# One decoder layer on one core: the rotation folded into q, projections through one bank, a third feed-forward bank, two-byte turns and another order of the stages

## Chip, cores and metric

One core of one Trainium2 chip runs the kernel alone. The metric is the device time of one execution in microseconds (us), as the median of several runs; lower is better.

## What is computed

Input x has 16 tiles of 128 tokens with 256 channels, in f32; a second input `ctx` has the same shape. Each tile goes through three parts, each followed by a layer norm of (input + part). Cut to what matters:

```python
# 1. attention over heads: for every token, its 16 heads attend to each other
q, k, v = (x @ w.T).reshape(b, s, 16, 16)          # for wq, wk, wv
q, k = apply_rope(q, inv_freq), apply_rope(k, inv_freq)
scores  = einsum('bshd,bstd->bsht', q, k) / 4      # per token s: heads h by heads t
attn    = einsum('bsht,bstd->bshd', softmax(scores), v) @ wo.T
# 2. wkv: a recurrence over the 128 tokens of a tile, with k = the normed x, v = ctx
y_t = (e1 * aa + e2 * v_t) / (e1 * bb + e2)        # aa, bb decay by exp(-exp(time_decay))
# 3. feed-forward with quantised activations (127 steps) and ternary weights, 256 -> 704 -> 256
h   = silu(bitlinear(x, w1)) * bitlinear(x, w2);  out = bitlinear(h, w3)
```

`apply_rope` turns the pairs of channels of a token by angles that depend on the token's place alone. q and k of one score belong to the same token, so they are turned by the same angles.

## The kernel before, in words

The program is written engine by engine: one in-order instruction list each for TensorE (`block.tensor`), ScalarE (`block.scalar`), GpSimd (`block.gpsimd`), VectorE (`block.vector`) and the DMA queue of SyncE (`block.sync`), with semaphores between them. All lists run the same outer loop, `run_steps` (L75): `STEPS` = 16 tiles + `DEPTH` 5 = 21 steps. In step s a stage written `on(at(d), stage)` works on tile s - d. The order of the `on` lines in each engine's `step` function is the order of its instructions in a step, and nothing else sets it; `due` starts one-time work (the rounding of the feed-forward weights to ternary) at its place in the first steps.

A tile goes through these stages:

- Attention. `project_qk` (L387) makes q and k, 512 columns, in the bank `ps_qk`; `project_v` (L396) makes v in `ps_vt`. `rope` (L857, VectorE) multiplies q and k by the cosines and by the sines, `rotate` (L708, GpSimd) takes the difference and the sum of these products into `qk_rot`, and `to_dmajor` (L866, VectorE) transposes it in 32x32 blocks, twice 512 columns. `copy_v` (ScalarE), `v_to_dmajor` (VectorE), `block_v` (TensorE, four turns) and `copy_v_blocks` (ScalarE) lay v out for the last product. `score` (L409) makes the scores of all heads of four tokens at once, with a mask in spare rows. `max_quads` and three small instructions find each row's maximum, `shift` (L431) subtracts it by matmuls, `exp_scores`, `weigh_v` (twice 16 small matmuls), `heads_to_tokens`, `recip_sums`, `normalise`, `turn_attn`, `copy_attn` and `project_out` finish. `residual`, `moments`, `mean_var` (VectorE), `inv_std` (L761, GpSimd, three instructions) and `layernorm` (ScalarE) are used for all three norms.
- Wkv. `turn_k`, `exp_k` (four ACTIVATEs), `weigh_past` and `weigh_now` (GpSimd), `scan` (L945, VectorE), `add_now` (GpSimd). The division is done for two neighbouring tokens at once: `pair_dens` (L740) multiplies their denominators, `recip_den` (L951, VectorE) takes 128 reciprocals a partition, `cross_terms` (L746) and `divide` (L752) multiply. `turn_y` gives it back.
- Feed-forward. `amax_of_x`, `floor_x`, `recip_x` (VectorE) and `ffn_scales` (GpSimd) give the scales. `scale_x` (ScalarE) adds the constant MAGIC, which rounds to whole numbers; `turn_xq` (L488, two f32 turns) and `copy_xq`, which takes MAGIC off again, give bf16. `up` (L495) makes gate and up values in `ps_a` and `ps_b`, in two halves of 352 columns; `tanh_gate`, `copy_up` (ScalarE), `gate_up` (L974, VectorE) and `hidden` (L771, GpSimd) follow for each half. `amax_of_h`, `floor_h`, `recip_h`, `scale_of_h`, `scale_of_out` (VectorE), `scale_h` (ScalarE), `turn_hq` (L508, six f32 turns into `ps_a` and `ps_b`), `copy_hq` (two ACTIVATEs) and `down` (L515, into `ps_b`) end it. `up` of the next tile waits for `residual` 2 of this one, which reads `ps_b`.

On SyncE, a step issues, in this order, the load of xT (for this step's tile), of ctx (for three tiles back), of x (one back) and the store of the result (five back); each waits until its buffer is free. The weights come before the loop and in step 1.

## Time and profile before

| | |
|---|---|
| median of 3 runs | 296.25 us (295.87 to 297.29) |
| the profiled execution, its own time | 293.11 us |
| its span, first to last instruction | 291.1 us |
| mean granted TensorE clock | 0.86 |
| TensorE busy (matmuls) | 223.6 us, 77% |
| VectorE busy | 228.6 us, 79% |
| GpSimd busy | 184.7 us, 63% |
| ScalarE busy | 163.2 us, 56% |

How to read it: all engines work at the same time, so the shares don't add up to the span. Busy is the time between an instruction's start and its end in the record; neighbouring records of one engine can overlap, so the time from one start to the next is what an instruction costs in the queue. PE is TensorE, PEld its weight loads, DVE is VectorE, ACT is ScalarE, POOL is GpSimd, SP is SyncE. TensorE's granted clock is 1.0 at 2.4 GHz and 0.5 at 1.2 GHz.

### The profile page before, as it was taken

The numbers are of one execution on the slowest core, as the hardware profiler recorded it, in microseconds if no ns is written. First come the engines' busy times: TensorE is split into PE (matmuls) and PEld (weight loads), VectorE is DVE, ScalarE is ACT, GpSimd is POOL, SyncE is SP. The second block draws the span as 40 slices with busy tenths as digits, with TensorE's granted clock in tenths as the row PEclk, the third lists the DMA queues.
The fourth block names the chain that finished last, engine by engine and source line by source line (L and its number), as shares of the span: only waits on it lengthen the run. The fifth ranks groups of instructions, "written<-read, shape, count | busy, mean of one in ns | idle before, by whom it ended". The sixth has DMA issues, their size and how long they took to land.

```text
span 291.1 us, 9999 instructions
## 1 busy us (share of the span) xinstructions
PE 223.6 (77%) x3778; PEld 151.4 (52%) x3778; DVE 228.6 (79%) x557; ACT 163.2 (56%) x345; POOL 184.7 (63%) x384
## 2 busy tenths in 40 slices
PE   3462996979989898999888989898988785553622
PEld 1341765656655656667656666666665553321211
DVE  2686466688999999999999999999999977564221
ACT  2206232446767768485858585767576756544341
POOL 2203116577797979696779778697979777774311
PEclk9859586889999999797999999999999979755555
DMA  7900101010020202020202020202011000100000
GB/s 210 334 0 2 38 5 52 24 35 23 2 69 9 74 2 78 2 74 2 74 3 75 3 74 3 74 2 74 25 55 39 21 21 18 37 1 20 0 18 18
DMA packets 11968, 12.34 MB, mean 42 GB/s; under 512 B 1872, under 2 KB 11152, under 8 KB 11920
## 3 DMA queue, kind: packets, MB, share of 16 engines
q1 hardware_dynamic: 11200, 11.67, 12.7%
q8 instruction: 30, 0.49, 0.7%
q14 instruction: 18, 0.15, 0.2%
q10 hardware_dynamic: 720, 0.03, 0.2%
HBM read 9.60 MB, written 2.10 MB: 40 GB/s over the span
## 4 chain that ended last, share of the span: by engine, by line
DVE 25%; PE 24%; issue 20%; POOL 17%; ACT 7%; DMA 3%; SPq 1%; DVEq 0%; POOLq 0%; ACTq 0%
PE ps_s L425 6%; POOL hid L775 5%; PE ps_b L518 5%; DVE quad_max L884 4%; DMA w_raw<-w_in 3%; POOL qk_rot L712 3%; DVE qkD L871 3%; POOL qk_rot L711 3%; DVE gate L978 3%; POOL rstd L766 3%; PE ps_qk L393 3%; DVE qk_cos L862 2%; PE ps_a L505 2%; PE ps_b L505 2%; DVE qk_sin L862 2%
## 5 line engine op out<-in xcount | busy, mean ns | idle before, releaser
L393 PE MATMUL ps_qk<-wqkv,xT 128*128 128x512 f32 x64 | 35.6, 686 | 4.8 <-DMA wqkv<-wqkv_in 4.8
L622 ACT ACTIVATE th<-ps_a,half_gate 128x352 f32<-128x352 f32 x32 | 17.7, 553 | 35.1 <-PE ps_b L505 35.1
L734 POOL TENSOR_TENSOR frac<-state,now 128x512 f32<-128x512 f32 x16 | 20.3, 1268 | 24.2 <-DVE state L948 24.2
L425 PE MATMUL ps_s<-qkD 20*64 20x64 f32 x1024 | 25.2, 242 | 10.8 <-DVE qkD L871 7.5
L775 POOL TENSOR_TENSOR hid<-gate,up_s 128x352 f32<-128x352 f32 x32 | 29.7, 931 | 3.7 <-ACT up_s L627 1.6
L425 PEld LDWEIGHTS ps_s<-qkD 20*64 20x64 f32 x1024 | 20.9, 150 | 16.4 <-DVE qkD L871 7.2
L766 POOL TENSOR_TENSOR rstd<-var_eps,minus_half 128x1 f32<-128x1 f32 x48 | 26.3, 549 | 3.8
L586 ACT ACTIVATE probs<-ps_s 128x512 f32<-128x512 f32 x32 | 18.6, 591 | 16.0 <-PE ps_s L440 16.0
L871 DVE STREAM_TRANSPOSE qkD<-qk_rot 128x512 f32<-128x512 f32 x32 | 20.9, 691 | 6.5 <-POOL qk_rot L712 5.5
L643 ACT ACTIVATE x<-res,nmr,rstd 128x256 f32<-128x256 f32 x32 | 19.3, 603 | 10.5 <-POOL nmr L768 10.5
L978 DVE SCALAR_TENSOR_TENSOR gate<-th,ps_a 128x352 f32<-128x352 f32 x32 | 16.1, 502 | 11.4 <-ACT th L622 11.4
L399 PE MATMUL ps_vt<-wqkv,xT 128*128 128x256 f32 x64 | 19.0, 421 | 5.6 <-ACT v_blk L580 5.6
L458 PE MATMUL ps_o<-probs,v_blk 64*32 64x64 f32 x1024 | 22.2, 227 | 1.0 <-ACT probs L586 0.9
L505 PE MATMUL ps_a<-w,xqT 128*128 128x352 bf16 x64 | 16.7, 347 | 7.6 <-DVE gate L978 4.2
L393 PEld LDWEIGHTS ps_qk<-wqkv,xT 128*128 128x128 f32 x64 | 13.6, 228 | 15.6 <-issue 14.1
L763 POOL TENSOR_TENSOR var_eps<-mv,eps 128x1 f32<-128x1 f32 x48 | 9.2, 191 | 19.6 <-DVE mv L940 19.1
L711 POOL TENSOR_TENSOR qk_rot<-qk_cos,qk_sin 128x256 f32<-128x256 f32 x16 | 11.5, 718 | 15.1 <-DVE qk_sin L862 15.1
L458 PEld LDWEIGHTS ps_o<-probs,v_blk 64*32 64x32 f32 x1024 | 17.1, 112 | 7.3 <-issue 6.9
L935 DVE BATCH_NORM_STATS2 stats<-res 128x6 f32<-128x256 f32 x48 | 20.3, 424 | 0.7
L440 PEld LDWEIGHTS ps_s<-neg_eye,max_hi 128*64 128x64 bf16 x512 | 17.4, 114 | 6.4 <-issue 6.4
L948 DVE TENSOR_TENSOR_SCAN state<-w_tab,past 128x516 f32<-128x516 f32 x16 | 20.5, 1280 | 0.1
L884 DVE TRANSPOSE_TENSOR_REDUCE quad_max<-ps_s 128x32 f32<-128x1024 f32 x16 | 19.8, 1240 | 0.5 <-PE ps_s L425 0.5
(115 smaller groups left out, 629.7 us busy)
## 6 DMA issues: line engine op xcount, KB each, us to landing
xT<-xT_in SPq DMA_DIRECT2D x16, 128.0 KB, 2.4
x_res<-x_in SPq DMA_DIRECT2D x16, 128.0 KB, 2.3
ctxT<-ctxT_in SPq DMA_DIRECT2D x16, 128.0 KB, 2.2
out<-y_out SPq DMA_DIRECT2D x16, 128.0 KB, 1.7
w_raw<-w_in SPq DMA_DIRECT2D x2, 704.0 KB, 7.1
wqkv<-wqkv_in SPq DMA_DIRECT2D x2, 384.0 KB, 4.0
w_raw<-w_in SPq DMA_DIRECT2D x1, 640.0 KB, 8.8
wo<-wo_in SPq DMA_DIRECT2D x1, 256.0 KB, 5.1
```

What stands on the lines that cost most here:

```text
L393: last = mm(ps_qk[:], xT[k.slot][:, h, :], wqkv[:, h, 0:2 * C], start=h == 0, stop=h == 1)
L425: last = mm(ps_s[64 * half:64 * half + 64, g % 2, col:col + BLK], kk, q, start=(g < 2 and b < 2), stop=False, skip_group_check=True)
L458: last = mm(ps_o[PAD * g:PAD * g + PAD, dst:dst + BLK], v_blk[k.slot][rows, jj, g, :], probs[rows, g % 2, src:src + BLK], start=True, stop ...
L505: last = mm(bank[:, 0:FH], xqT[:, h, :], w12[:, h, i, cols], start=h == 0, stop=h == 1)
L734: g.tensor_tensor(frac[:].rearrange("p i h n -> p (i h) n"), state[:].rearrange("p i h n -> p (i h) n")[:, :, 0:P], now[:].rearrange("p i ...
L766: g.tensor_tensor(rstd[i][:], var_eps[i][:], minus_half[:], ALU.pow).then_inc(rstd_done[i], 1)
L775: g.tensor_tensor(hid[:, half * FH:(half + 1) * FH], gate[half][:], up_s[half][:], ALU.mult).then_inc(hid_done, 1)
L871: last = v.transpose(qkD[k.slot][:, i].rearrange("p (y h l) -> p h y l", h=HEADS, l=2), by_head[:, i])
L884: v.tensor_reduce(quad_max[:].rearrange("p s c -> p (s c)"), ps_s[:].rearrange("p b (c x) -> p (b c) x", x=PAD), AX.X, ALU.max, apply_tran ...
L935: v.bn_stats(stats[i][:], res[i][:]).then_inc(stats_done[i], 1)
L948: v.tensor_tensor_scan(flat(state), flat(w_tab), flat(past), 0.0, ALU.mult, ALU.add).then_inc(scanned, 1)
L978: v.scalar_tensor_tensor(gate[half][:], th[half][:], 1.0, ps_a[:, 0:FH], ALU.add, ALU.mult).then_inc(gate_done, 1)
```

## The change

What it does, by part:

- Rotation. Turning q and k by the same angles multiplies their product by cos^2 + sin^2 of each channel pair. `turn_gain` holds that factor per token and channel, `copy_q` (VectorE) multiplies q by it while copying it out of the bank, and k is only copied. `rope`, `rotate` and the tiles `qk_cos`, `qk_sin`, `qk_rot` go.
- One bank `ps_qkv` for q (256 columns), then k and v (512 columns), then the turned v blocks, in turn. ScalarE copies k and v together. All three are transposed on VectorE as before, now as three instructions in three places.
- Wkv: `pair_dens` and `cross_terms` go, `recip_den` takes 256 reciprocals a partition, and `divide` is one product.
- A third feed-forward bank `ps_c` holds the turned h and the result of `down`. `up` 0 waits for `copy_up` 1 and (through `turn_xq`) `gate_up` 1 of the tile before, and `turn_hq` for its `residual` 2.
- `whole_x` and `whole_h` (GpSimd) take MAGIC off into bf16, and the turns of xq and hq move bf16. `copy_xq` and `copy_hq` are plain copies, the second in one ACTIVATE.
- `DEPTH` 6: 22 steps. The stages stand in another order in all five lists, with other tile offsets.
- The DMA of the pads goes last on ScalarE's queue, and waits on constants moved from before the loops into the first tile of the stages that need them. Some counting semaphores are split in two.

The diff, cut:

```diff
-U_CUT = 50.0
+U_CUT = 60.0
-DEPTH = 5
+DEPTH = 6
...
-            def project_qk(k):
+            def project_q(k):
                 wait(pe, ld_xT[k.slot], 16 * (k.pair + 1))
-                wait(pe, rope_products, k.t)
+                wait(pe, v_blocks, k.t)
...
+                    last = mm(ps_q, xT[k.slot][:, h, :], wqkv[:, h, 0:C], start=h == 0, stop=h == 1)
+                last.then_inc(q_projected, 1)
+
+            def project_kv(k):
+                wait(pe, q_copied, k.t + 1)
                 for h in range(HALVES):
-                    last = mm(ps_v, xT[k.slot][:, h, :], wqkv[:, h, 2 * C:3 * C], start=h == 0, stop=h == 1)
-                last.then_inc(v_projected, 1)
+                    last = mm(ps_kv, xT[k.slot][:, h, :], wqkv[:, h, C:3 * C], start=h == 0, stop=h == 1)
+                last.then_inc(kv_projected, 1)
...
             def block_v(k):
-                wait(pe, v_dmajor, k.t + 1)
+                wait(pe, v_turned, k.t + 1)
+                wait(pe, kv_copied, k.t + 1)
...
             def turn_xq(k):
-                wait(pe, x_scaled, k.t + 1)
-                wait(pe, hqT_ready, k.t)
+                wait(pe, x_whole, k.t + 1)
+                wait(pe, gate_done[1], k.t)
                 for h in range(HALVES):
-                    last = turn(ps_a[:, h * P:(h + 1) * P], xq32[:, h * P:(h + 1) * P])
+                    last = mm(ps_xq[:, h * P:(h + 1) * P], xq16[:, h * P:(h + 1) * P], ident16[:],
+                              start=True, stop=True, is_transpose=True)
...
             def up(k, half):
                 if half == 0:
                     wait(pe, xqT_ready, k.t + 1)
-                    wait(pe, res_done[2], k.t)
+                    wait(pe, up_copied[1], k.t)
...
             def turn_hq(k):
-                wait(pe, h_scaled, k.t + 1)
+                wait(pe, h_whole, k.t + 1)
+                wait(pe, res_done[2], k.t)
...
             def down(k):
...
-                    last = mm(ps_b[:, 0:C], hqT[:, c, :], w3[:, c, :], start=c == 0, stop=c == FCH - 1)
+                    last = mm(ps_c[:, 0:C], hqT[:, c, :], w3[:, c, :], start=c == 0, stop=c == FCH - 1)
...
-            def rotate(k):
-                wait(pool, rope_products, k.t + 1)
-                wait(pool, qk_dmajor, k.t)
-                g.tensor_tensor(qk_rot[:, :, 0:HH], qk_cos[:, :, 0, :], qk_sin[:, :, 1, :], ALU.subtract)
-                g.tensor_tensor(qk_rot[:, :, HH:HD], qk_sin[:, :, 0, :], qk_cos[:, :, 1, :],
-                                ALU.add).then_inc(rotated, 1)
...
+                g.tensor_tensor(yT[:], frac[:, 1], den_rec[:], ALU.mult).then_inc(y_ready, 1)
...
+            def whole_h(k):
+                wait(pool, h_scaled, k.t + 1)
+                wait(pool, hq_turned, k.t)
+                g.tensor_scalar(hq16[:, 0:HIDDEN], hq32[:], -MAGIC, 1.0, ALU.add, ALU.mult).then_inc(h_whole, 1)
...
-            def rope(k):
-                wait(dve, qk_projected, k.t + 1)
-                wait(dve, rotated, k.t)
-                src = ps_qk[:].rearrange("p (g i) -> p g i", i=HH)
-                for dst, tab in ((qk_cos, cos_t), (qk_sin, sin_t)):
...
+            def copy_q(k):
...
+                wait(dve, q_projected, k.t + 1)
+                wait(dve, q_dmajor, k.t)
+                v.tensor_tensor(qkv_tok[:, 0, :, 0:HD].rearrange("p h (a i) -> p h a i", i=HH),
+                                ps_q.rearrange("p (h a i) -> p h a i", a=2, i=HH),
+                                turn_gain[:].unsqueeze(1).unsqueeze(1).broadcast_to([P, HEADS, 2, HH]),
+                                ALU.mult).then_inc(q_copied, 1)
...
             def recip_den(k):
-                wait(dve, pairs_done, k.t + 1)
+                wait(dve, frac_done, k.t + 1)
                 wait(dve, y_ready, k.t)
-                v.reciprocal(den_rec[:], den_pair[:]).then_inc(den_recips, 1)
+                v.reciprocal(den_rec[:], frac[:, 0]).then_inc(den_recips, 1)
```

The new order of a step, each list from first to last, with the tile offset in brackets (one-time work left out; its places: FFN weights' DMA in step 0; weight sums in VectorE's step 1 behind the transpose of k, TensorE's sum in step 2 ahead of the scores, the scales at the end of VectorE's step 1, rounding in ScalarE's step 1, cuts in VectorE's step 2, ternary weights in GpSimd's step 2):

- TensorE: project_kv (1), project_out (3), shift (2), block_v (1), turn_xq (5), weigh_v 0 (2), up 0 (5), weigh_v 1 (2), project_q (0), turn_hq (6), turn_y (4), up 1 (5), down (6), turn_k (3), score (1), turn_attn (2)
- VectorE: mean_var 1 (4), copy_q (0), gate_up 1 (5), q_to_dmajor (0), residual 2 (6), max_quads (1), amax_of_x (4), max_rows (1), floor_x (4), max_hi_part (1), recip_x (4), max_lo_part (1), scan (3), turn_v (0), amax_of_h (5), residual 0 (2), floor_h (5), recip_h (5), moments 0 (2), scale_of_h (5), mean_var 0 (2), recip_den (3), k_to_dmajor (0), gate_up 0 (4), moments 2 (6), heads_to_tokens (1), mean_var 2 (6), residual 1 (3), recip_sums (1), moments 1 (3), scale_of_out (5), normalise (1)
- ScalarE: copy_kv (0), scale_x (4), exp_scores 0 and 1 (1), copy_xq (4), copy_v_blocks (0), scale_h (5), tanh_gate 0 (4), copy_up 0 (4), copy_hq (5), layernorm 0 (2), tanh_gate 1 (4), copy_up 1 (4), layernorm 2 (6), exp_k (2), layernorm 1 (3), copy_attn (1)
- GpSimd: hidden 1 (5), weigh_past (3), weigh_now (3), whole_x (4), add_now (3), ffn_scales (4), inv_std 0 (2), whole_h (5), divide (3), hidden 0 (4), inv_std 2 (6), inv_std 1 (3)
- SyncE: xT (-1, the next tile's), store (6), x (0), ctx (1)

## Rows read from the trace of the kernel before

**Rows 1.** stretches: us, busy PE PEld DVE ACT POOL, PEclk, DMA share, GB/s.

```profile
176.03:189.72 13.69, 12.44 (x237) 8.45 (x236) 13.29 (x35) 9.70 (x22) 11.16 (x24) 1.00 0.13 41
259.00:273.00 14.00, 6.63 (x25) 3.37 (x24) 6.00 (x17) 5.88 (x11) 6.34 (x16) 0.50 0.03 11
```

**Rows 2.** timeline of VectorE, one middle step: start us, us, instruction.

```profile
177.33 0.42 DVE L935 BATCH_NORM_STATS2 stats<-res 128x6 f32<-128x256 f32 x1
177.66 0.48 DVE L896 CAST max_hi<-row_max 128x16 bf16<-128x16 f32 x1
...
178.55 0.94 DVE L954 RECIPROCAL den_rec<-den_pair 128x128 f32<-128x128 f32 x1
...
179.44 0.67 DVE L862 TENSOR_TENSOR qk_cos<-ps_qk,cos_t 128x512 f32<-128x512 f32 x1
...
180.64 0.50 DVE L978 SCALAR_TENSOR_TENSOR gate<-th,ps_a 128x352 f32<-128x352 f32 x1
181.06 0.41 DVE L923 TENSOR_TENSOR res<-ps_o,x_res 128x256 f32<-128x256 f32 x1
181.51 0.43 DVE L935 BATCH_NORM_STATS2 stats<-res 128x6 f32<-128x256 f32 x1
181.97 0.18 DVE L940 BATCH_NORM_AGGREGATE mv<-stats 128x2 f32<-128x6 f32 x1
182.23 0.89 DVE L984 TENSOR_REDUCE amax_h<-hid 128x1 f32<-128x704 f32 x1
183.16 0.21 DVE L991 TENSOR_SCALAR c_h<-amax_h,s_h 128x1 f32<-128x1 f32 x1
183.40 0.16 DVE L996 RECIPROCAL rec_h<-c_h 128x1 f32<-128x1 f32 x1
183.48 0.42 DVE L926 TENSOR_TENSOR res<-ps_w,x 128x256 f32<-128x256 f32 x1
183.82 0.20 DVE L1001 TENSOR_SCALAR s_h<-rec_h,s_h 128x1 f32<-128x1 f32 x1
```

**Rows 3.** VectorE's groups, whole run: busy us, mean ns of one | idle before.

```profile
L954 DVE RECIPROCAL den_rec<-den_pair 128x128 f32<-128x128 f32 x16 | 15.1, 941 | 0.0
...
L910 DVE RECIPROCAL o_rec<-o_tok 128x16 f32<-128x16 f32 x16 | 3.8, 236 | 0.0
```

**Rows 4.** timeline of TensorE, the middle step before that.

```profile
170.41 0.44 PE L385 MATMUL ps_w<-ident,x 128*128 128x128 f32 x2 [0.74 <-ACT x L643]
...
172.48 0.69 PE L425 MATMUL ps_s<-qkD 20*64 20x64 f32 x32 [0.20 <-DVE qkD L871]
...
174.00 0.83 PE L518 MATMUL ps_b<-w,hqT 128*128 128x256 bf16 x6
174.86 0.44 PE L385 MATMUL ps_a<-ident,xq 128*128 128x128 f32 x2
175.14 0.60 PE L385 MATMUL ps_vt<-ident,vD 128*128 128x128 f32 x4
```

**Rows 5.** GpSimd's groups, whole run.

```profile
L711 POOL TENSOR_TENSOR qk_rot<-qk_cos,qk_sin 128x256 f32<-128x256 f32 x16 | 11.5, 718 | 15.1 <-DVE qk_sin L862 15.1
...
L744 POOL TENSOR_TENSOR den_pair<-frac 128x128 f32<-128x128 f32 x16 | 6.4, 399 | 0.1
...
L794 POOL TENSOR_SCALAR w<-w_raw 128x1408 bf16<-128x1408 f32 x2 | 2.7, 1363 | 2.2 <-DVE w_raw L1026 2.2
```

**Rows 6.** VectorE's score maxima 1, 5, 16, residuals 2 of the last two tiles.

```profile
19.09 1.25 DVE L884 TRANSPOSE_TENSOR_REDUCE quad_max<-ps_s 128x32 f32<-128x1024 f32 x1
...
78.10 1.24 DVE L884 TRANSPOSE_TENSOR_REDUCE quad_max<-ps_s 128x32 f32<-128x1024 f32 x1
...
230.69 1.24 DVE L884 TRANSPOSE_TENSOR_REDUCE quad_max<-ps_s 128x32 f32<-128x1024 f32 x1
...
271.93 0.48 DVE L930 SCALAR_TENSOR_TENSOR res<-ps_b,s_out,x 128x256 f32<-128x256 f32 x1 [2.02 <-PE ps_b L518]
...
285.91 0.48 DVE L930 SCALAR_TENSOR_TENSOR res<-ps_b,s_out,x 128x256 f32<-128x256 f32 x1 [5.19 <-PE ps_b L518]
```

More of the change, by code:

```diff
@@ L84, in on, with once @@
         stage(tile, *which)
-class Due:
-    def __init__(self):
-        self.begun = set()
-    def __call__(self, what, tile):
-        if tile is None or what in self.begun:
-            return False
-        self.begun.add(what)
-        return True
+def once(tile, stage, *which):
+    if tile is not None and tile.t == 0:
+        stage(*which)
 def decoder_layer(nc, x_in, xT_in, ctxT_in, wqkv_in, wo_in, w1_in, w2_in, w3_in,
@@ L364, in load_ffn_weights @@
                 sp.dma_start(w3_raw[0:HIDDEN - full * P, full, :], w3_in[full * P:HIDDEN, :]).then_inc(ld_ffn, 16)
[L366 removed]
             def step(at):
[L369 to L374 removed]
+                on(at(-1), load_xT)
+                on(at(6), store)
+                once(at(0), load_ffn_weights)
+                on(at(0), load_x)
+                on(at(1), load_ctx)
             run_steps(step)
@@ L1035, in weight_scales @@
                     v.tensor_scalar(dst[:], wmean[:, i:i + 1], s, None, ALU.mult).then_inc(w_scales, 1)
-            due = Due()
             def step(at):
+                once(at(0), wkv_tables)
+                on(at(4), mean_var, 1)
+                on(at(0), copy_q)
+                on(at(5), gate_up, 1)
+                on(at(0), q_to_dmajor)
+                on(at(6), residual, 2)
+                on(at(1), max_quads)
+                once(at(2), cut_weights, 0)
+                on(at(4), amax_of_x)
```

395 lines of the change are left out of this document (186 added, 209 removed).

## The prediction

> **What bounds the kernel now.** I read the profile's page first, then the stretches, then one step of VectorE. By the page VectorE has the largest share of the span, but only 79%; the stretches show why. From the fifth score maximum at 78.1 us to the sixteenth at 230.7 us [rows 6] lie 11 steps in 152.6 us, 13.87 each. At full granted clock a step takes 13.69 us, and VectorE is busy for 13.29 of them; TensorE 12.44, GpSimd 11.16, ScalarE 9.70 [rows 1]. So the middle belongs to VectorE, with TensorE 0.85 us behind it. Outside it no engine is full: from 259 to 273 us VectorE works 6.00 of 14, at a TensorE clock of 0.50 (1.2 GHz) [rows 1], and yet a step takes 14.0 us (271.93 to 285.91) [rows 6]. There a chain across engines sets the step.
>
> The step of VectorE [rows 2] shows that busy is not all work. An instruction whose successor doesn't need it hands over before its own end: residual 1 to the scale of h 0.34 us from start to start. The same form followed by its own reader takes 0.45 (residual 0 to its moments). Moments to the next 0.33 where it is free, 0.46 to their own mean; mean 0 to the maximum of h 0.26 for an instruction of 0.18; maximum of h to its floor 0.93 for one of 0.89; floor to reciprocal 0.24. With moments 1, the score maximum ahead of its row maximum and the last small one before the transposes these are eight places, 0.1 to 0.2 each: some 1.0 us of the 13.69 is reader behind writer.
>
> **Part by part, for one tile in the middle.** Times are start to start unless said otherwise.
>
> Rotation: cos and sin products leave VectorE (1.20 for both, 179.44 to 180.64) [rows 2]. One product of half the columns comes. From the same kind of source 512 columns take 0.60 and 352 (the gate, 180.64 to 181.06) 0.42, so 1.1 ns a column, and 256 take 0.31; the residual of 256 columns takes 0.34 free and 0.45 ahead of its reader [rows 2]. Bounds 0.31 and 0.45. I take 0.33: its reader stands one instruction further on. The three 32x32 transposes stay. Net -0.87.
>
> Wkv denominators: den_pair and both cross products leave GpSimd, but the reciprocal on VectorE goes from 128 to 256 columns. A reciprocal takes 941 ns for 128 columns and 236 for 16 [rows 3], so 6.3 ns a column: +0.80. Bounds +0.70 (941 less all of the 236) and +0.89 (the whole of 178.55 to 179.44 once more) [rows 2]. I take the slope of the rows, 0.80. The Trainium skill (VectorE: DVE Perf Modes, in its paragraph on why there are 8 slices) says that the reciprocal is an iterative divide with a repeat count of 8; with the 0.96 GHz of the same page that would be, as an estimate, 8.3 ns a column and +1.07, and the total 4 us higher (279). The measured slope of 6.3 ns does not agree with it.
>
> Order: residual 0, moments 0 and mean 0 now alternate with floor, reciprocal and scale of h; residual 1, moments 1 and mean 1 with reciprocals, moments 2 and others; the score maximum with the maximum of x. Of the eight places only floor-to-reciprocal of h and parts of two more stay. I take 0.8 of the 1.0 as gained; bounds 0 and 1.0.
>
> VectorE's step is then 13.69 - 0.87 + 0.80 - 0.80 = 12.8 us. Without the order it would be 13.6: the rotation and the reciprocal cancel.
>
> TensorE: its waits in the step are 0.74 and twice 0.20 (one of them shown) [rows 4], which leaves 12.6 us of work in 13.69. q, k and v are the same columns in another split: nothing. Two turns of xq take 0.28 (174.86 to 175.14), so the six of hq 0.84; they will move 2-byte data. Six bf16 matmuls of 256 columns take 0.86 (174.00 to 174.86), so by columns 0.07 for 128: the eight turns 0.56 instead of 1.12; bounds of the gain 0 (a turn stays at 0.14) and 0.56, and I take 0.56, the type being the same. So 12.0 us, 0.8 under VectorE.
>
> GpSimd: less two halves of the rotation (0.72 each), den_pair (0.40) and two crosses, no shorter; plus xq and hq less the magic number, whose form (to bf16) took 1.36 us for 1408 columns [rows 5], so 0.3 for 256 and 0.7 for 704. 11.2 - 2.6 + 1.0 = 9.6 us at most. ScalarE: a larger copy of k and v for that of v, one copy of hqT for two: about even at 9.7. Both are far under 12.8 and hidden; whole_h is so only until turn_hq is due, behind which stand turn_y, up 1, down and the scores. Split semaphores, U_CUT and the four small table instructions (about 0.2 each, while the first projection and the pads are under way) cost nothing; without that cover, 0.8 once.
>
> Does the order fit 12.8? I laid one step out with the durations of the groups, VectorE's list from zero. copy_q ends at 0.5, max_lo at 4.1, turn_v at 5.9, scale of h at 7.8, reciprocal of the denominators 7.9 to 9.6, transpose of k 10.2, gate 0 10.6, attn 12.9. TensorE: the scores' shift at 4.8, block_v at 5.9 (waits 0.2), q at 8.5, turn_hq at 9.9 (scale 7.9 to 8.9 on ScalarE, inverse deviation then whole_h on GpSimd until 9.8: waits 0.4), up 1 at 10.9, down 11.5, scores 12.7 to 14.2, turn_attn 14.2, next k and v 14.6. VectorE needs these scores at 14.7 and down's output at 14.3: both in time by 0.3 or more. The ring through the one bank (q, copy_q, kv, copy_kv, turn_v, block_v, copy_v_blocks) is 6 us of work and has its waits where VectorE has other work. SP: a store waits for the last norm of its step, and x, ctx and the next xT stand behind it, half a step or more ahead of their use; ctx is asked for two steps ahead. So 12.8 holds with TensorE close behind. I add 0.1 for hops that the layout misses, and 0.18, by which the mean of the 11 intervals of before exceeds 13.69: 13.1. Eleven steps: 11 x (13.1 - 13.87) = -8.5 us.
>
> Head: five score maxima start at 19.1 to 78.1 us [rows 6]. There the chain counts: projection, two products, 1.4 us of rotation on GpSimd, transposes, scores, maximum; the next projection queues behind it. The rotation's hop goes. Laid out with the same durations at the half clock, the first maximum is later (20.8: kv waits for copy_q, copy_kv and the pads' DMA, now last on ScalarE's queue; scores stand behind the next q), but the weights' sums now run beside TensorE's work of tile 1, and the next come at 33, 46, 57 and 68. That is -10; I take -8, since layouts err to the short side. More DMAs do not come: xT of tile 1 goes ahead of the FFN weights by 0.5 us of issue, and these are summed 10 us after they land.
>
> Tail: from the last maximum to the span's end 60.4 us, in four steps of 13.8 and 5.2 behind the last residual 2 (285.91) [rows 6]. Before, the up-projection of a tile waits for the previous residual 2 (one bank for both) and so a whole FFN is one step. The third bank parts them: up 0 of the next tile needs only gate 1 and copy_up 1. DEPTH 6 makes it five steps and 5.2, but the layout gives 9.9 each: 54 to 55. Against it, the 256-column reciprocal (+0.8) and whole_x, whole_h (+1.2) are in the last tile's chain. I take -5.
>
> Sum: 293.1 (span 291.1 and 2.0 around it) - 8.5 - 8 - 5 = 271.6. The median of the runs shown is 3.1 us above this execution, so **275 us**.
>
> **Rivals.** B, the places between VectorE's instructions stay or become waits for TensorE, which is 0.8 behind: a step of 13.5 to 13.7. For it: TensorE's layout has only 0.3 to spare, and the two maxima waiting for scores would pass it on. Against it: in the middle no VectorE instruction waits today for TensorE. Head and tail keep 8 and 5, the middle 2: 293.1 - 15 + 3.1 = 281, up to 288 where the head gains little. C, same time: B, and the sixth step eats what the ends gain, 293 to 298. D, slower: a chain across queues keeps every step at 13.7, as it does in the tail today with VectorE 43% busy. Its place is turn_hq: scale_h, whole_h behind the inverse deviation on GpSimd, turn_hq, copy_hq, down, residual 2. Then the sixth stage costs a step in the tail: 5 x 13.7 + 5.2 = 73.7 instead of 60.4, and head and middle stay: 296 + 13 = 309. It decides from 11.1 us a step in the tail ((60.4 - 5.2) / 5), and in the middle from a wait at turn_hq of 1.5 us (12.0 + 0.2 + 1.5 = 13.7); I find 0.4. That the change doesn't do what it says can be left out: the instructions that go are gone from the lists of all tiles.
>
> **Numbers.** Forecast 0.56 (own range 266 to 280), lower still 0.05, B 0.24, C 0.06, D 0.09. Faster by over 0.5% 0.85, within 0.5% (about what a measurement of this kernel can tell from no change) 0.06, slower 0.09. The range leaves out D, C and the lowest, 0.20: 266 to 290. Its low end has the middle at 12.6 flat (all of the 1.0 gained, nothing added: -14) and the whole layout of the ends (-10, -6), its high end B with a head that gains nothing.
>
> **What would show it.** In the changed profile: score maxima 13.0 to 13.2 us apart in the middle; the reciprocal of 256 columns at 1.7 us; one product of 256 columns at 0.4; turns of bf16 at about 0.07 start to start; waits of VectorE for TensorE under 0.3 a step; fifth maximum at 68 to 71 us; 54 to 56 us behind the last. The forecast is wrong if VectorE shows a wait for the scores or for down in every step, if TensorE waits over 1 us for hq16, or if the tail's steps stay at 13.7.

## The result and the profile after

| | before | after |
|---|---|---|
| median, same chip | 296.06 us (4 runs) | 262.66 us (4 runs, 262.2 to 263.07) |
| the profiled execution, its own time | 293.11 us | 262.2 us |
| its span | 291.1 us | 260.4 us |
| TensorE, VectorE busy | 77%, 79% | 80%, 84% |

The ratio is 0.887 (0.883 to 0.892): 11% faster. The forecast was 275 us with a range of 266 to 290. The sign was right, but the time lies under the whole range.

The profile's page of after (engines' busy time, then the granted clock in 40 slices of the span) and its stretches (columns as in [rows 1]), one middle step and the first from residual 2 to residual 2 in the tail:

```profile
PE 208.2 (80%) x3778; PEld 139.9 (54%) x3778; DVE 217.7 (84%) x544; ACT 160.9 (62%) x329; POOL 161.5 (62%) x336
...
PEclk9986869999999999999999999999999757555665
```

```profile
91.36:103.73 12.37, 11.59 (x238) 8.14 (x238) 12.34 (x33) 9.46 (x21) 9.64 (x21) 1.00 0.15 46
...
201.74:214.71 12.97, 11.60 (x192) 8.36 (x193) 10.97 (x28) 8.40 (x18) 10.53 (x22) 0.62 0.11 33
```

The span fell by 30.7 us. By the score maxima (next block, against [rows 6]), the head to the fifth maximum gave 11.7 us (78.10 to 66.38), the eleven middle steps 16.5 (152.6 to 136.08) and the tail 2.5 (60.4 to 57.9). A middle step takes 12.37 us instead of 13.69 [rows 1], VectorE is busy for 12.34 of it, and the granted clock is 1.0 in all of it.

VectorE's timeline of after (start us, us, instruction; [rows 2] answers to the step, [rows 6] to the score maxima and the residual):

```profile
20.54 1.25 DVE L869 TRANSPOSE_TENSOR_REDUCE quad_max<-ps_s 128x32 f32<-128x1024 f32 x1 [1.25 <-PE ps_s L429]
...
66.38 1.23 DVE L869 TRANSPOSE_TENSOR_REDUCE quad_max<-ps_s 128x32 f32<-128x1024 f32 x1
...
91.36 1.23 DVE L869 TRANSPOSE_TENSOR_REDUCE quad_max<-ps_s 128x32 f32<-128x1024 f32 x1
92.52 0.38 DVE L946 TENSOR_REDUCE amax_x<-x 128x1 f32<-128x256 f32 x1
...
93.03 0.21 DVE L881 CAST max_hi<-row_max 128x16 bf16<-128x16 f32 x1
93.15 0.15 DVE L959 RECIPROCAL s_x<-c_x 128x1 f32<-128x1 f32 x1
93.27 0.18 DVE L885 TENSOR_TENSOR max_lo<-row_max,max_hi 128x16 bf16<-128x16 f32 x1
...
97.06 1.73 DVE L941 RECIPROCAL den_rec<-frac 128x256 f32<-128x256 f32 x1
98.72 0.65 DVE L858 STREAM_TRANSPOSE qkD<-qkv_tok 128x512 f32<-128x512 f32 x1
...
102.00 0.39 DVE L842 TENSOR_TENSOR qkv_tok<-ps_qkv,turn_gain 128x256 f32<-128x256 f32 x1
...
202.46 1.25 DVE L869 TRANSPOSE_TENSOR_REDUCE quad_max<-ps_s 128x32 f32<-128x1024 f32 x1 [0.24 <-PE ps_s L429]
...
255.19 0.48 DVE L915 SCALAR_TENSOR_TENSOR res<-ps_c,s_out,x 128x256 f32<-128x256 f32 x1 [4.55 <-PE ps_c L528]
```

The maxima 1, 5 and 16 stand at 20.54, 66.38 and 202.46. In the step no instruction shows a wait. Between most writers and their readers stands another instruction now: the score maximum of 1.23 us gives way after 1.16 to the maximum of x. The reciprocal of 256 columns takes 1.73 us and 1.66 to the next; the one product of q 0.31.

The cast to `max_hi`, which took 0.40 us from start to start before [rows 2], takes 0.12. That is not the order's doing alone. First VectorE's timeline of before, one step ahead of [rows 2], then GpSimd's in the same step, then GpSimd's in after:

```profile
163.98 0.48 DVE L896 CAST max_hi<-row_max 128x16 bf16<-128x16 f32 x1
...
168.55 0.89 DVE L984 TENSOR_REDUCE amax_h<-hid 128x1 f32<-128x704 f32 x1
```

```profile
161.72 1.27 POOL L734 TENSOR_TENSOR frac<-state,now 128x512 f32<-128x512 f32 x1 [1.57 <-DVE state L948]
...
163.91 0.51 POOL L749 TENSOR_TENSOR cross<-frac 128x128 f32<-128x128 f32 x1
...
166.62 1.89 POOL L775 TENSOR_TENSOR hid<-gate,up_s 128x352 f32<-128x352 f32 x2
```

```profile
92.48 0.73 POOL L713 TENSOR_TENSOR now<-now,ctxT 128x256 f32<-128x256 f32 x1
```

Before, the cast starts behind the start of a cross product and ends 0.04 us after it (164.46 and 164.42); in after it starts late in the product `now` and again ends 0.03 after it (93.24 and 93.21). So what the cast lost is a hold by GpSimd, and it went with the cross products and their place.

TensorE's timeline of after, one middle step and then the tail ([rows 4] answers to the first part):

```profile
96.34 0.65 PE L462 MATMUL ps_o<-probs,v_blk 64*32 64x64 f32 x32 [0.33 <-DVE res L908]
...
99.34 0.51 PE L521 MATMUL ps_c<-ident,hq 128*128 128x128 bf16 x6
100.03 0.44 PE L379 MATMUL ps_w<-ident,yT 128*128 128x128 f32 x2 [0.18 <-POOL yT L729]
...
100.90 0.82 PE L528 MATMUL ps_c<-w,hqT 128*128 128x256 bf16 x6
...
102.76 0.69 PE L429 MATMUL ps_s<-qkD 20*64 20x64 f32 x32 [0.20 <-PE ps_s L429]
...
231.04 0.39 PE L498 MATMUL ps_a<-ident,xq 128*128 128x128 bf16 x2 [3.97 <-POOL xq L765]
...
251.90 0.82 PE L521 MATMUL ps_c<-ident,hq 128*128 128x128 bf16 x6 [5.16 <-POOL hq L770]
```

In the step TensorE waits 0.33, 0.18 and 0.20 us, 0.71 in all. In the tail it waits for GpSimd's whole-number copies of x and h: 3.97 and 5.16 us. Each wait is for the whole chain that ends in such a copy; the copies themselves take 0.68 us (of x, 230.31) and 0.78 (of h, 251.06).

### The profile page after: what moved, and what is told of

The parts are those of the page before. It is cut to its first block, busy times and chain, and to the rows that moved or that the text cites. A ratio compares the mean times of both kernels' runs of the same rounds, so it can differ in the third digit from the quotient of the medians.

```text
span 260.4 us, 9989 instructions
## 1 busy us (share of the span) xinstructions
PE 208.2 (80%) x3778; PEld 139.9 (54%) x3778; DVE 217.7 (84%) x544; ACT 160.9 (62%) x329; POOL 161.5 (62%) x336
## 2 busy tenths in 40 slices
DMA packets 11968, 12.34 MB, mean 47 GB/s; under 512 B 1872, under 2 KB 11152, under 8 KB 11920
## 3 DMA queue, kind: packets, MB, share of 16 engines
q1 hardware_dynamic: 11200, 11.67, 14.5%
## 4 chain that ended last, share of the span: by engine, by line
PE 50%; DVE 22%; issue 18%; ACT 4%; POOL 3%; DMA 1%; DVEq 1%; POOLq 0%; ACTq 0%
PE ps_qkv L393 13%; PE ps_s L429 9%; PE ps_o L476 5%; PE ps_w L379 4%; DVE amax_h L972 4%; PE ps_c L528 4%; DVE vT L863 3%; PE ps_a L514 3%; DVE qkD L858 3%; PE ps_b L514 3%; DVE gate L965 2%; DVE den_rec L941 2%; PE ps_o L379 2%; DVE wsum L1009 2%; PE ps_o L462 2%
## 5 line engine op out<-in xcount | busy, mean ns | idle before, releaser
L393 PE MATMUL ps_qkv<-wqkv,xT 128*128 128x512 f32 x64 | 35.5, 683 | 1.9 <-DVE qkv_tok L842 1.9
L941 DVE RECIPROCAL den_rec<-frac 128x256 f32<-128x256 f32 x16 | 27.7, 1733 | 0.0
L429 PE MATMUL ps_s<-qkD 20*64 20x64 f32 x1024 | 23.9, 234 | 3.3 <-PE ps_s L429 3.3
L577 ACT ACTIVATE qkv_tok<-ps_qkv 128x512 f32<-128x512 f32 x16 | 9.6, 598 | 25.3 <-PE ps_qkv L393 25.3
L387 PE MATMUL ps_qkv<-wqkv,xT 128*128 128x256 f32 x64 | 19.8, 431 | 6.1 <-DMA wqkv<-wqkv_in 5.3
L429 PEld LDWEIGHTS ps_s<-qkD 20*64 20x64 f32 x1024 | 19.8, 143 | 8.1 <-PE ps_s L429 5.1
L660 ACT ACTIVATE hqT<-ps_c 128x768 bf16<-128x768 bf16 x16 | 13.0, 811 | 16.4 <-PE ps_c L521 16.4
L623 ACT ACTIVATE th<-ps_a,half_gate 128x352 f32<-128x352 f32 x32 | 17.5, 548 | 5.6 <-PE ps_b L514 4.9
L721 POOL TENSOR_TENSOR frac<-state,now 128x512 f32<-128x512 f32 x16 | 19.0, 1185 | 1.5 <-DVE state L935 1.5
L920 DVE BATCH_NORM_STATS2 stats<-res 128x6 f32<-128x256 f32 x48 | 19.4, 405 | 0.2
L444 PE MATMUL ps_s<-neg_eye,max_hi 128*64 128x64 bf16 x512 | 19.5, 200 | 0.1
```

What stands on the lines that cost most here:

```text
L387: last = mm(ps_q, xT[k.slot][:, h, :], wqkv[:, h, 0:C], start=h == 0, stop=h == 1)
L393: last = mm(ps_kv, xT[k.slot][:, h, :], wqkv[:, h, C:3 * C], start=h == 0, stop=h == 1)
L429: last = mm(ps_s[64 * half:64 * half + 64, g % 2, col:col + BLK], kk, q, start=(g < 2 and b < 2), stop=False, skip_group_check=True)
L444: last = mm(o, m, neg_eye[:, half, :], start=False, stop=part is max_lo, skip_group_check=True)
L920: v.bn_stats(stats[i][:], res[i][:]).then_inc(stats_done[i], 1)
L941: v.reciprocal(den_rec[:], frac[:, 0]).then_inc(den_recips, 1)
```

## The experiments

Two theories stood at first. **Theory 1**: VectorE's in-order list is what sets the middle, so every tenth taken out of it or put into it comes back in the step. **Theory 2**: beside it lies a ring of nearly the same length through other engines, that is, a chain of stages, each waiting for the one before, that comes back to its own start one step later. Each time below is the median against the kernel before on the same chip (294.61, 295.11, 295.89 and 295.32 us for the four groups).

### Readers right behind their writers again (a_adj)

```diff
@@ after, VectorE's step (the pattern) @@
                 on(at(1), max_quads)
-                on(at(4), amax_of_x)
                 on(at(1), max_rows)
-                on(at(4), floor_x)
                 on(at(1), max_hi_part)
...
+                on(at(4), amax_of_x)
+                on(at(4), floor_x)
```

> The changed kernel with VectorE's list alone re-ordered: each reader right behind its writer again (score maximum, row maximum and its two halves; maximum of x, floor, reciprocal; maximum of h, floor, reciprocal, scale; residual, moments and mean of norm 0; residual and moments of norms 1 and 2 near each other). Theory 1 (the step in the middle is VectorE's list from start to start, and the new order took out the places where a reader stood behind its writer): these come back, about 0.9 us a step, so maxima 13.2 to 13.3 us apart instead of 12.37, and 274 to 278 us in all. Rival (the order helps because it parts the chains between engines, and VectorE's own places cost nothing): under 265 us.

289.97 us (287.09 to 292.57), 27 us more than after. Its middle step takes 14.22 us. VectorE's timeline:

```profile
126.24 1.23 DVE L869 TRANSPOSE_TENSOR_REDUCE quad_max<-ps_s 128x32 f32<-128x1024 f32 x1
127.51 0.19 DVE L876 TENSOR_REDUCE row_max<-quad_max 128x16 f32<-128x32 f32 x1
127.73 0.38 DVE L881 CAST max_hi<-row_max 128x16 bf16<-128x16 f32 x1
...
140.46 1.24 DVE L869 TRANSPOSE_TENSOR_REDUCE quad_max<-ps_s 128x32 f32<-128x1024 f32 x1
```

The same instructions as in after, and no wait for another engine is shown in the step (126.24 to 140.46). The maximum holds its reader for 1.27 us (1.16 in after), the cast for 0.41 (0.12). Twelve writers with their reader right behind them each take 0.10 to 0.15 us more than in after, 1.45 us in all, and the cast 0.29; with 0.1 of small differences elsewhere that is 1.85 us, the difference of the steps. Some 0.2 of the cast's 0.29 is again GpSimd: it ends at 128.11, the product `now` beside it at 128.08. So theory 1 holds on this side of the balance. The size was missed by half (expected 0.9 a step and 274 to 278 us): one place costs what I had given it, 0.1 to 0.2 us, but this list has thirteen of them.

### Paired denominators back (a_pair)

```diff
@@ after @@
-                v.reciprocal(den_rec[:], frac[:, 0])
+                v.reciprocal(den_rec[:], den_pair[:])
@@ GpSimd's step @@
                 on(at(3), add_now)
+                on(at(3), pair_dens)
+                on(at(3), cross_terms)
```

> The changed kernel with the paired denominators of before: VectorE takes 128 reciprocals a partition instead of 256 (0.8 us less a step), GpSimd has the pair product and two cross products again (1.3 us more, ahead of the feed-forward scales). Theory 1 (VectorE's list sets the middle): VectorE falls to 11.55, TensorE with 11.6 busy and some waits takes over at 11.8 to 12.1, so 256 to 260 us. Rival (VectorE is no longer alone: a chain or TensorE sets 12.37 already, or GpSimd's 1.3 us arrive late at the feed-forward): 262 us or more.

272.24 us (270.41 to 275.37), and 12.89 a step: 0.52 longer than after, although VectorE has 0.8 us less to do. It now waits 1.12 us a step for the turn of y, which comes behind GpSimd's two further stages. A miss for theory 1. At least with GpSimd's list in this order, the long reciprocal is no price but the cheaper way.

### The rotation alone (b_rot)

```diff
@@ before, VectorE and GpSimd @@
-                for dst, tab in ((qk_cos, cos_t), (qk_sin, sin_t)):
-                    last = v.tensor_tensor(dst, src, tab, ALU.mult)
+                v.tensor_tensor(qk_rot[:, 0:HEADS], ps_qk[:, 0:C], turn_gain, ALU.mult)
-                on(at(1), rotate)
@@ ScalarE @@
+                on(at(0), copy_k)
```

> The kernel before with the rotation alone changed: VectorE multiplies q by one factor (256 columns), ScalarE copies k behind it, GpSimd's two halves of the rotation go; order, banks, depth and turns as before. Theory 1: VectorE's step 13.69 - 0.87 = 12.8, TensorE's 12.6 of work right under it, so 12.9 to 13.1 in the middle; in the head one hop of 1.5 us less a step: 276 to 284 us. Rival (the gain of the change is its order and banks, and the rotation was covered): 292 us or more.

290.65 us (289.35 to 291.96), ratio 0.987 (0.980 to 0.993). VectorE's timeline:

```profile
144.07 1.23 DVE L952 TENSOR_TENSOR_SCAN state<-w_tab,past 128x516 f32<-128x516 f32 x1 [0.27 <-issue]
...
150.07 0.52 DVE L982 SCALAR_TENSOR_TENSOR gate<-th,ps_a 128x352 f32<-128x352 f32 x1 [0.23 <-ACT th L628]
...
152.17 0.89 DVE L988 TENSOR_REDUCE amax_h<-hid 128x1 f32<-128x704 f32 x1 [0.57 <-POOL hid L775]
...
157.71 1.23 DVE L952 TENSOR_TENSOR_SCAN state<-w_tab,past 128x516 f32<-128x516 f32 x1
```

GpSimd's, and the step as a stretch:

```profile
145.38 1.28 POOL L734 TENSOR_TENSOR frac<-state,now 128x512 f32<-128x512 f32 x1 [1.40 <-DVE state L952]
...
150.30 1.84 POOL L775 TENSOR_TENSOR hid<-gate,up_s 128x352 f32<-128x352 f32 x2
```

```profile
145.93:159.57 13.64, 12.55 (x238) 8.53 (x236) 12.57 (x33) 9.62 (x23) 9.79 (x22) 1.00 0.15 41
```

A step takes 13.64 us, against 13.69 [rows 1], with 0.9 us less on VectorE. The time came back as waits: 0.23 for the tanh ahead of gate 1, 0.57 for the hidden product. No engine is full in this step. The median lies between what the theories gave (276 to 284, and 292 or more), but the step is the one that theory 1 cannot bear and theory 2 can: in the kernel before, a ring was already as long as VectorE's list.

The rows show which one. The scan (144.07) releases GpSimd's sum `frac` (145.38), and from there GpSimd goes through its list without a wait for another engine: sums, scales, pair and cross products, an inverse deviation, the division and both hidden products, until 152.14. The maximum of h starts at 152.17, and 5.54 us of VectorE's list later stands the next scan (157.71): 8.10 + 5.54 = 13.64. In the kernel before it is 8.14 (174.09 to 182.23) and 5.55 (to 187.78), 13.69. The cos and sin products stood beside GpSimd's 8 us, so their going brings nothing. This ring does not go through a feed-forward bank.

### Rotation and the long reciprocal (b_rot_rec, and again b_rot_rec2)

```diff
@@ b_rot @@
-                v.reciprocal(den_rec[:], den_pair[:])
+                v.reciprocal(den_rec[:], frac[:, 0])
@@ GpSimd's step @@
-                on(at(3), pair_dens)
-                on(at(3), cross_terms)
```

> The one before plus the reciprocal of 256 columns without pairing, everything else as in the kernel before. Theory 1: +0.80 us a step on VectorE, so 13.6 us in the middle, where rotation and reciprocal cancel as the prediction has it, and 287 to 292 us with the head's gain. Rival (the reciprocal lies beside other work): within 2 us of the run with the rotation alone.

> The kernel before with the rotation as one factor and one reciprocal of 256 columns: VectorE's part of the change without any of the order. The prediction's sentence (rotation and reciprocal cancel, 13.6 without the order): 13.6 a step, 291 to 295 us. Theory 2 with the ring's way through GpSimd, which is now free of the paired product and the cross terms: also 13.6. If the reciprocal stands in the ring itself (it holds the rotation, the gate 1 and all that follow in the list by 0.8 us): 14.2 to 14.5 a step, 298 to 305 us.

310.35 us (303.3 to 312.58) and 311.78 (306.18 to 312.2), a spread too wide for a ratio; both medians are above what was expected (at most 292 and 305). The second one's VectorE, first in a step at a lower clock, then in the next, at full clock:

```profile
158.87 0.52 DVE L959 SCALAR_TENSOR_TENSOR gate<-th,ps_a 128x352 f32<-128x352 f32 x1 [1.04 <-ACT th L624]
159.30 1.75 DVE L935 RECIPROCAL den_rec<-frac 128x256 f32<-128x256 f32 x1
...
172.84 0.16 DVE L877 CAST max_hi<-row_max 128x16 bf16<-128x16 f32 x1
...
177.90 0.89 DVE L965 TENSOR_REDUCE amax_h<-hid 128x1 f32<-128x704 f32 x1 [0.88 <-POOL hid L754]
```

The two feed-forward halves stand on either side of the reciprocal in the old list: gate 0 at 158.87 waits 1.04 us, and then 1.75 us of reciprocal pass before gate 1 can come. From maximum to maximum (155.82 to 171.12) it is 15.30 us at a mean granted clock of 0.89. The next step (171.12 to 185.30) has full clock and takes 14.18 us, as such steps do in both runs; the eleven steps of the middle take 15.0 and 15.2 on the mean, at 0.89 and 0.85.

So the prediction's sentence that the two would cancel and leave 13.6 is wrong by 0.5 to 0.6 at full clock, inside what was expected of a reciprocal in the ring (14.2 to 14.5), and by 1.4 to 1.6 on the mean, with the lower clock, which was in no sum. By busy time they cancel, by place they don't: GpSimd's division waits for the reciprocal, and behind it stand the hidden products and the maximum of h, which waits 0.88 us for them. The cast takes 0.16 us here instead of 0.48: the cross products beside it are gone.

### Half of the reciprocals left out (a_half_rec)

```diff
@@ after @@
-                v.reciprocal(den_rec[:], frac[:, 0])
+                v.reciprocal(den_rec[:, :, 0:P // 2], frac[:, 0, :, 0:P // 2])
```

> The changed kernel, where VectorE takes the reciprocal of only the first 64 tokens of a tile (128 columns instead of 256); the other denominators are left at 1 and GpSimd does nothing more. It takes the same 0.8 us off VectorE as the pairing did, without the 1.3 us on GpSimd. Theory 2 (VectorE's list sets 12.37, and the pairing lost because its products stand on GpSimd ahead of the inverse deviation, whole_h and the division): 11.7 to 12.0 us a step, up against TensorE's 11.6 busy, and 254 to 257 us. Rival (a ring through the other engines already lies at 12.3): 261 to 263 us.

261.55 us (260.14 to 263.21), ratio 0.885 (0.878 to 0.891), 12.28 a step. VectorE's timeline:

```profile
130.58 1.24 DVE L870 TRANSPOSE_TENSOR_REDUCE quad_max<-ps_s 128x32 f32<-128x1024 f32 x1
...
139.80 0.42 DVE L912 TENSOR_TENSOR res<-ps_w,x 128x256 f32<-128x256 f32 x1 [0.51 <-PE ps_w L379]
...
142.86 1.24 DVE L870 TRANSPOSE_TENSOR_REDUCE quad_max<-ps_s 128x32 f32<-128x1024 f32 x1
```

0.8 us off VectorE, 0.09 off the step: VectorE waits 0.51 for the turn of y and smaller bits elsewhere. In after as well, then, the two limits lie on top of each other: VectorE's list at 12.37 and a path through the turn of y at 12.28.

### One product more on VectorE (a_vload)

```diff
@@ after, VectorE's step @@
                 on(at(5), gate_up, 1)
+                on(at(5), load)          # scratch, 512 columns
```

> The changed kernel with one more instruction in VectorE's list, a product of two scratch tiles of 512 columns behind the gate of half 1, which nobody waits for (0.55 to 0.6 us start to start). Theory 2: all of it lands in the step: maxima 12.9 to 13.0 us apart, 270 to 273 us. Rival (VectorE has slack behind other engines): under 265 us.

271.27 us (269.29 to 272.04), 12.94 a step: +0.57. What is put into VectorE's list is paid in full, what is taken out brings next to nothing.

### One product more on GpSimd, where it waits (a_fill)

```diff
@@ after, GpSimd's step @@
                 on(at(3), weigh_now)
+                on(at(3), fill)          # scratch, 256 columns
                 on(at(4), whole_x)
```

> The changed kernel with one more instruction on GpSimd, a product of two scratch tiles of 256 columns in the 1.2 us in which it waits for xq, which nobody waits for. Theory 2a (the small cast of the row maximum costs VectorE 0.12 us here against 0.40 in the kernel before because GpSimd stands still beside it): the cast goes back to 0.3 to 0.4 and the step to 12.6, 265 to 268 us, though GpSimd has room. Rival (the cast is short for another reason, such as its place): the cast stays at 0.12 and the time within 1 us of the changed kernel.

268.56 us (267.65 to 269.35), 12.84 a step: +0.47. First VectorE's timeline, then GpSimd's, then GpSimd's in after:

```profile
95.14 0.21 DVE L887 CAST max_hi<-row_max 128x16 bf16<-128x16 f32 x1
...
95.38 0.65 DVE L891 TENSOR_TENSOR max_lo<-row_max,max_hi 128x16 bf16<-128x16 f32 x1
95.95 1.22 DVE L941 TENSOR_TENSOR_SCAN state<-w_tab,past 128x516 f32<-128x516 f32 x1
```

```profile
95.28 0.73 POOL L765 TENSOR_TENSOR scratch<-scratch 128x256 f32<-128x256 f32 x1
96.50 0.87 POOL L770 TENSOR_SCALAR xq<-xq 128x256 bf16<-128x256 f32 x1 [0.50 <-ACT xq L612]
```

```profile
94.40 0.41 POOL L765 TENSOR_SCALAR xq<-xq 128x256 bf16<-128x256 f32 x1 [1.19 <-ACT xq L611]
```

The product lies in GpSimd's wait and ends before xq is there, so by the lists it costs nothing. But max_lo, 16 columns, takes 0.65 us instead of 0.18, and delays the scan by 0.48; and whole_x takes 0.87 beside the scan instead of 0.41. max_lo ends at 96.03, the product beside it at 96.01. The cast, on which I had bet, kept its 0.21, but this run does not test it: the product starts 0.14 us behind the cast, and what the cast meets is `now`, as in after.

### xq turned in f32 (a_xq32)

```diff
@@ after @@
-                    last = mm(ps_xq[...], xq16[...], ident16[:], is_transpose=True)
+                    last = turn(ps_xq[...], xq32[...])
-                on(at(4), whole_x)
```

> The changed kernel with xq turned in f32 as before: whole_x goes from GpSimd, the copy takes the constant off, turn_hq stays in two bytes. Theory 2: TensorE has slack in the middle, so its 0.14 us cost nothing there; a hop of 0.45 us goes from each tile's chain in head and tail: 260 to 263 us. Rival (TensorE is as much the bound as VectorE, so its turns count): 264 to 266 us.

262.37 us (261.28 to 263.26), ratio 0.888 (0.883 to 0.893), 12.37 a step: the same. The two-byte turn of xq brings no time. What it does for h can't be undone alone: six f32 turns of 128 columns don't fit into the one bank that `ps_hq` has.

### Another order of VectorE's list in the kernel before (b_order, b_rot_order)

```diff
@@ before (b_order) and b_rot (b_rot_order), VectorE's step @@
                 on(at(0), rope)
+                on(at(2), residual, 0)
                 on(at(4), gate_up, 1)
-                on(at(2), residual, 0)
                 on(at(2), moments, 0)
-                on(at(2), mean_var, 0)
                 on(at(4), amax_of_h)
+                on(at(2), mean_var, 0)
                 on(at(4), floor_h)
-                on(at(4), recip_h)
                 on(at(3), residual, 1)
+                on(at(4), recip_h)
```

> The kernel before with only VectorE's list put in another order: moments 2 and mean 2 go into the gaps of the score maximum, residual 0 ahead of gate 1, and moments 0, maximum of h, mean 0, floor, residual 1, reciprocal, moments 1, scale of h, mean 1 alternate. Six of the eight places where a reader stands right behind its writer go, about 0.7 us of VectorE's 13.7. Theory 1 (VectorE's list alone sets the middle, every tenth taken out of it counts): 13.0 to 13.1 us a step, 286 to 288 us. Theory 2 (a ring through TensorE, ScalarE, VectorE's gate and GpSimd's hidden product of equal length lies beside the list): 13.5 to 13.65 a step, 292 to 295 us, and VectorE shows waits of about 0.5 us at the gate or at the maximum of h.

> The kernel before with the rotation as one factor and with that order of VectorE's list, so that VectorE has 1.5 us a step less to do: both banks of the feed-forward, the old lists of TensorE, ScalarE and GpSimd and the paired denominators stay. Theory 1: 12.1 to 12.3 a step, 274 to 278 us. Theory 2: 13.4 to 13.6 a step, 288 to 291 us, the same as with the rotation alone (290.65), with VectorE idle for over 1 us of a step.

339.1 us, ratio 1.141 (1.137 to 1.146), and 329.93 us, ratio 1.111 (1.107 to 1.115). Both theories missed. (The profile of b_order is of an execution of 646 us and is not read.) One step of b_rot_order, as a stretch and on TensorE:

```profile
162.06:178.86 16.80, 14.67 (x238) 10.66 (x237) 12.56 (x33) 9.82 (x23) 10.15 (x22) 0.80 0.12 34
```

```profile
173.19 0.44 PE L385 MATMUL ps_w<-ident,x 128*128 128x128 f32 x2 [1.93 <-ACT x L649]
```

Mean 0 now stands behind the maximum of h, which itself waits for the hidden product. GpSimd's inverse deviation and ScalarE's norm 0 come later for it, and TensorE, in order, waits 1.93 us for `turn_k` with everything behind it. The step is 16.80 us at a granted clock of 0.80, and VectorE is busy for 12.56. Of the 3.16 us over b_rot's step, TensorE idles 1.04 (2.13 against 1.09) and is busy 2.12 longer (14.67 against 12.55) with the same work. The gaps that the order saves are worth some tenths; a stage moved behind one that waits cost microseconds here, the lower clock included.

### The third bank taken away (a_two, a_two_late)

```diff
@@ after (a_two) @@
-        ps_hq = ps_c[:].bitcast(BF16)
+        ps_hq = ps_b[:].bitcast(BF16)
             def up(k, half):
                 if half == 0:
+                    wait(pe, res_done[2], k.t - 1)
                 else:
+                    wait(pe, hqT_ready, k.t)
             def turn_hq(k):
-                wait(pe, res_done[2], k.t)
+                wait(pe, up_copied[0], min(k.t + 2, TILES))
             def down(k):
+                wait(pe, up_copied[1], min(k.t + 2, TILES))
@@ a_two_late: turn_hq behind up 1 instead, copy_hq behind copy_up 1 @@
```

> The kernel after with two feed-forward banks instead of three: the turns of hq and the output of down share the bank of the up values, so the second up half waits for the copy of hq, down for the copy of the second up half, and up of the tile after the next for residual 2. Everything else, order included, stays. Theory 2 (the third bank is what breaks the ring, and the order needs it): 13.2 to 14.5 a step, 272 to 285 us, with TensorE waiting for the copies in every step. Rival (the order alone is enough; the bank pays only in the last steps): 12.4 to 12.6 a step in the middle, and 3 to 6 us more in the tail, 266 to 270 us.

> The kernel after with two feed-forward banks, but arranged as the kernel before has it: on TensorE the second up half goes ahead of the turns of hq and of down, on ScalarE the copy of hq behind the second copy of up, and up of a tile waits for residual 2 of the tile two before. VectorE's list with all of its interleaving, the single rotation factor, the shared projection bank and the 256-column reciprocal stay. Theory 2 (a ring up 0, gate 0, up 1, copy, turns of hq, down, residual 2 through the two banks sets the step whatever VectorE's list is): 13.3 to 14.5 a step in the middle and 283 to 298 us. Rival (the two banks were only badly arranged in the run before this one; VectorE's list decides): 12.4 to 12.9 a step, 266 to 273 us.

a_two: 297.63 us, ratio 1.004 (1.001 to 1.007), above the 272 to 285 expected. Its profile is of an execution of 302.5 us, and I read one of its steps at full clock. First that step as a stretch, then TensorE in it:

```profile
160.01:173.92 13.91, 11.82 (x237) 8.01 (x238) 12.52 (x32) 9.61 (x21) 9.65 (x21) 1.00 0.13 41
```

```profile
169.46 0.46 PE L515 MATMUL ps_a<-w,xqT 128*128 128x352 bf16 x2 [0.37 <-ACT hqT L662]
...
171.31 0.82 PE L530 MATMUL ps_b<-w,hqT 128*128 128x256 bf16 x6 [1.09 <-ACT up_s L630]
```

13.91 us a step with all other parts of the change in place: the 11% are gone. Three of the eleven middle steps take that and one 14.27 at full clock; seven take 15.1 to 15.4 us at clocks of 0.88 to 0.90, and the mean is 14.81 at 0.93. TensorE waits 0.37 for the copy of hq and 1.09 for the second copy of up, and VectorE is busy for 12.52 of 13.91. a_two_late, with two banks arranged as before, took 328.95 us (ratio 1.117), 17.5 a step at a clock of 0.80 and also above what was expected (283 to 298), and TensorE in it:

```profile
165.22 0.49 PE L521 MATMUL ps_b<-ident,hq 128*128 128x128 bf16 x6 [1.09 <-ACT up_s L628]
166.62 1.46 PE L528 MATMUL ps_b<-w,hqT 128*128 128x256 bf16 x6 [0.90 <-ACT hqT L660]
```

It waits 1.09 for the bank and 0.90 for the copy, at a lower clock: six matmuls of `down` take 1.46 us, in after 0.82 (100.90). In both TensorE waits for the copies out of the shared banks, as theory 2 has it; the rival, that the bank pays in the last steps only, falls. What is shown is that the new order needs the bank. That the bank without the new order would bring anything is not: a_adj has the bank and takes 14.22 a step, longer than before, and no run puts the third bank alone into the kernel before.

## Why the prediction was wrong

**Direction of the change of order: right.** VectorE's places behind a writer went, and after has no wait in its list.

**The step that failed: "VectorE's step is then 13.69 - 0.87 + 0.80 - 0.80 = 12.8 us", raised to 13.1.** Its terms, as measured: rotation -0.89 (1.20 to 0.31), reciprocal +0.77 (0.89 to 1.66), both right. The term for the order, -0.80, was too small: the rest is 13.69 - 0.89 + 0.77 - 12.37 = 1.20. Of it 0.28 is the cast (0.40 to 0.12), which GpSimd's cross product had held and which was in no term; 0.92 is left for the order and for the small waits that went with it, near the 1.0 that I saw and took down to 0.8. The further 0.28 that I added for hops and for the stretches at a lower clock were not there: the granted clock is 1.00 over the stretch from 66 to 200 us. Together 0.7 us a step, 8 us over eleven steps, of the 12 by which 275 was too high.

**The path that it had wrong: "Both are far under 12.8 and hidden", of GpSimd and ScalarE.** By busy time that is so, but GpSimd's list from the sum behind the scan to the hidden products lay in a ring of 13.69 us, as long as VectorE's list (b_rot). One of my eight places was its mark: mean 0 to the maximum of h, 0.26 us, is no reader behind its writer but a wait for the hidden products, which end 0.04 us ahead of it (168.51 and 168.55). So the rotation alone gave 0.05 a step, not 0.87, and the gains could not be banked one by one. It did no harm to the forecast only because the change took this ring apart: pair and cross products are gone, and the two halves of a tile's hidden product no longer stand in a row right ahead of its maximum. That is read from the lists and from after's step without a wait; no run shows it by itself.

**"Without the order it would be 13.6: the rotation and the reciprocal cancel": wrong**, 14.18 at full clock and 15.0 and 15.2 on the mean (b_rot_rec, b_rot_rec2).

**"The third bank parts them", credited in the tail with -5: the place was wrong.** The middle needs it: 13.91 a step at full clock without it, 12.37 with it. It needs the order as much (14.22 in a_adj). In the tail the change gave 2.5. My layout had 9.9 us a step from the first; the first two took 12.25 and 12.13, as TensorE still had 11.60 us of work in 12.97 at a clock of 0.62. `whole_x` and `whole_h` take 0.7 and 0.8 us there, near the 1.2 that I had given them. Without whole_x (a_xq32) the tail from the sixteenth maximum (203.59) to the end of the span (259.8) is 56.2 us instead of 57.9; the tails of the other runs close to after lie between 57.0 and 58.4.

**Head**: first, second and fifth maximum laid out at 20.8, 33 and 68, found at 20.5, 33.9 and 66.4. Taking 2 off the layout's 10 ("layouts err to the short side") was over half of the error here: -11.7 instead of -8.

**Costed at little, and so it was**: TensorE's two-byte turns (six of hq 0.51 us, 99.34; a_xq32 shows no difference in time); TensorE's work 12.37 less 0.71 of waits, 11.7 (I had 12.0); GpSimd 9.64 (at most 9.6). The Trainium skill's repeat count of 8 (VectorE: DVE Perf Modes, in its paragraph on why there are 8 slices) would have given, as an estimate, 8.3 ns a column; the rows give (1733 - 941) / 128 = 6.2.

**Rivals.** B came closest in kind, though after shows no such wait: VectorE waits for TensorE only with half the denominators taken out, where the step is still 0.1 us under after's, and in a_pair. D's place was `turn_hq`; it waits there only in the tail. What the rivals lacked was one on the fast side, where the result lay: I had given it 0.05.

The terms of the miss: middle 8.0 us, head 3.7, tail -2.5, and 2.6 of the 3.1 that I had added between this execution and the median, where after has 0.5 (262.66 over 262.2). That is 11.8 of 12.3 (275 - 262.66); the rest is rounding up to 275 and the 2.0 around the span, which is 1.8.

**Open**: how short a step with two banks can be made. My two arrangements were worse than the kernel before, so they show that these lists need the third bank, not that no list with two comes near. What the third bank, the sixth step of depth or the single projection bank does by itself was not tried either. No run beats after clearly; a_half_rec and a_xq32 are within its scatter.

## What to carry to other kernels

An engine that is 97% busy can have a ring of the same length beside it. Before you bank what comes off its list, add up the rings that go through other engines' lists and through shared buffers, or take one thing away and look whether a wait takes its place. An instruction that starts a few hundredths after another engine's work ends may be waiting, even where no wait is shown. Order pays in two ways of very different size: about a tenth for each reader that no longer stands right behind its writer, microseconds for a stage that stands between two members of a ring.

## What the runs showed of the hardware

- **A reader right behind its writer costs VectorE 0.10 to 0.15 us**, 1.45 us for twelve such places in a step (a_adj against after, the same 32 instructions). An instruction that needs nothing of the one ahead starts 1.16 us after a start of 1.23 (91.36, 92.52), the reader 1.27 after it (126.24, 127.51). The Trainium skill (VectorE: DVE Perf Modes, The DRAIN you can't avoid) says that the next operation does not start until the pipeline is empty, that one which is not held starts earlier, and that in a chain of copies semaphores between operations cost nothing extra. The trace agrees with the earlier start; the last does not carry over to these pairs, whose reader waits for a semaphore of its writer.
- **GpSimd and VectorE hold each other.** max_lo took 0.65 instead of 0.18 us while a GpSimd product ran, whole_x 0.87 instead of 0.41 beside the scan, the cast 0.48 behind the start of a cross product and 0.16 without one (b_rot_rec2). The held one ends just after the other: max_lo and the cast 0.02 to 0.04 us after the product, whole_x 0.20 after the scan (97.37 and 97.17). The Trainium skill (GPSIMD Engine Reference, Specifications) says that the two contend for their shared memory interfaces where a VectorE instruction has two SBUF inputs or runs in a two-port mode; max_lo and the scan have two inputs, and the trace agrees. The cast has one, and no trace shows its mode. An idle GpSimd is not free room.
- **A longer wait of TensorE and a lower clock came together, and the clock cost more than the wait**: in b_rot_order 1.93 us of wait in a step stand beside a granted clock of 0.80 and 14.67 us of TensorE's busy time, for work that takes 12.55 in b_rot at full clock. Against b_rot's step of 13.64 the idle time grew by 1.04 us, the busy time by 2.12. That the waits bring the clock down is not shown: a_two, with the same lists throughout, has steps of 13.91 us at full clock beside steps of 15.2 at 0.89.
